# Scans of two head pairs back to back in odd steps, and their decays requested and cleared two at a time

## The reference

```python
xn = layernorm(x)
proj = xn @ in_proj_w.T                        # gate, xBC, dt
xBC = silu(causal_conv4(xBC) + conv_b)         # x (8192 channels), B and C (8 groups of 128)
# scan in chunks of 128 tokens, 128 heads of 64 channels, 16 heads a group
cs = cumsum(dt * A)
scores = einsum('bclhn,bcshn->bchls', C, B) * where(tri, exp(cs_l - cs_s), 0)
y = scores @ (x * dt) + (part from the chunk before) + D * x
yg = y * silu(gate)
out = (yg * rsqrt(mean(yg**2 over a group) + eps)) * norm_w @ out_proj_w.T
return x + out * silu(expert_ffn(xn))
```

## Time and profile before

| | us |
|---|---|
| median of 3 runs (lowest, highest) | 1611.23 (1611.13, 1611.86) |
| profiled execution, its own time | 1611.21 |
| its span | 1609.3 |
| PE busy | 1589.1 |
| DVE busy | 1410.1 |
| ACT busy | 1196.8 |
| POOL busy | 960.9 |

### The profile page before, as it was taken

The page is one execution under the profiler, slowest core; times in us unless marked ns, Lnnn a source line. Parts: engine busy times, 40 slices in busy tenths (PEclk is TensorE's granted clock), DMA queues, the critical chain, the costliest instruction groups (busy, mean ns, idle before and its releaser), DMA issues.

```text
span 1609.3 us, 28461 instructions
## 1 busy us (share of the span) xinstructions
PE 1589.1 (99%) x8478; PEld 1268.0 (79%) x8478; DVE 1410.1 (88%) x1654; ACT 1196.8 (74%) x2305; POOL 960.9 (60%) x596
## 2 busy tenths in 40 slices
PE   9999989999999999999999999999999999999998
PEld 6888768877778777877778777877778777877776
DVE  7726899889898899889898899889998899889987
ACT  4525878777887878777887878777887778778772
POOL 6522456656666656655665656656666656656563
PEclk9999999999999999999999999999999999999999
DMA  5234344434443444434443444334443444434432
GB/s 187 80 130 142 117 142 149 138 113 138 141 152 108 150 133 147 138 114 148 138 144 119 138 134 149 136 115 158 135 139 124 132 134 156 130 120 155 151 132 84
DMA packets 83831, 216.88 MB, mean 135 GB/s; under 512 B 10576, under 2 KB 12880, under 8 KB 83536
## 3 DMA queue, kind: packets, MB, share of 16 engines
q1 hardware_dynamic: 83376, 214.55, 39.7%
q10 hardware_dynamic: 288, 0.30, 0.1%
HBM read 209.83 MB, written 4.98 MB: 133 GB/s over the span
## 4 chain that ended last, share of the span: by engine, by line
PE 86%; DVE 7%; issue 3%; ACT 3%; POOL 1%; DMA 0%; ACTq 0%; DVEq 0%; POOLq 0%; SPq 0%
PE pj L454 15%; PE pj L456 15%; PE pj L455 15%; PE pr L454 9%; PE pr L455 8%; PE pr L456 8%; PE sc L677 7%; PE tb L666 3%; PE sc L681 3%; DVE conv L1335 2%; DVE wo_lo L1399 1%; ACT decay L936 1%; DVE xc L1349 1%; PE tb L690 1%; PE pr L655 1%
## 5 line engine op out<-in xcount | busy, mean ns | idle before, releaser
L1036 POOL TENSOR_TENSOR w_lo<-stg,w_hi 128x512 fp32r<-128x512 f32 x316 | 496.2, 1571 | 322.7 <-ACT w_hi L910 261.4
L454 PE MATMUL pj<-xT_hi,w_hi 128*128 128x512 f32 x1208 | 477.4, 395 | 9.6 <-DVE conv L1335 5.3
L456 PE MATMUL pj<-xT_hi,w_lo 128*128 128x512 f32 x1208 | 471.4, 390 | 0.0
L455 PE MATMUL pj<-xT_lo,w_hi 128*128 128x512 f32 x1208 | 471.0, 390 | 0.0
L1335 DVE SCALAR_TENSOR_TENSOR conv<-pj,par,conv 128x510 f32<-128x510 f32 (+2 forms) x480 | 357.8, 745 | 77.6 <-ACT conv L918 64.4
L936 ACT ACTIVATE decay<-decay,dtg 128x256 f32<-128x256 f32 (+1 forms) x1024 | 379.0, 442 | 0.0
L1073 POOL TENSOR_TENSOR xc<-xc,thg 128x512 f32<-128x512 f32 x128 | 203.1, 1587 | 188.1 <-DVE xc L1386 187.5
L1079 POOL TENSOR_TENSOR sqsum<-sqsum,sq 128x512 f32<-128x512 f32 x112 | 218.1, 1947 | 113.9 <-ACT sq L962 110.5
L454 PEld LDWEIGHTS pj<-xT_hi,w_hi 128*128 128x128 f32 x1208 | 226.9, 188 | 65.5 <-issue 13.5
L456 PEld LDWEIGHTS pj<-xT_hi,w_lo 128*128 128x128 f32 x1208 | 226.9, 188 | 47.9
L455 PEld LDWEIGHTS pj<-xT_lo,w_hi 128*128 128x128 f32 x1208 | 227.1, 188 | 45.1
(11 more groups left out here) (180 smaller groups left out, 1993.2 us busy)
## 6 DMA issues: line engine op xcount, KB each, us to landing
stg<-wstream SPq DMA_DIRECT2D x387, 256.0 KB, 2.7
decay<-cs_scr SPq DMA_DIRECT2D x128, 768.0 KB, 4.3
acc<-hid SPq DMA_DIRECT2D x8, 256.0 KB, 4.6
out<-acc SPq DMA_DIRECT2D x8, 256.0 KB, 2.0
dt_scr<-decay SPq DMA_DIRECT2D x1, 1024.0 KB, 6.5
gate_scr<-part SPq DMA_DIRECT2D x4, 256.0 KB, 2.0
dtg<-dt_scr SPq DMA_DIRECT2D x16, 64.0 KB, 4.5
stg<-hid SPq DMA_DIRECT2D x4, 256.0 KB, 4.5
```

What stands on the lines that cost most here:

```text
L454: nc.tensor.matmul(dst, hi_w, hi_x, start=first, stop=False)
L455: nc.tensor.matmul(dst, hi_w, lo_x, start=False, stop=False)
L456: return nc.tensor.matmul(dst, lo_w, hi_x, start=False, stop=last)
L1036: nc.gpsimd.tensor_tensor(w_dest(n, 1), stg[:, s % RING, :], f32(w_dest(n, 0)), ALU.subtract).then_inc(S["wl"], 1)
```

## The change

PE scans in odd steps only: pair s-1 and pair s back to back. Even pairs still go to the bank `sc`; odd ones go to `tb` (pair 1), `pr[0]` (3) and `pr[3]` (5 and 7), with the waits this needs. In step 1 `x_turn` of pair 2 moves to the end of the step, since `tb` holds pair 1's result. SP requests the decays of pairs s+2 and s+3 in even steps, behind the step's weight tiles. ACT does `drops` of an even pair behind the tap and the second weight split of the even step, and `y_hi` and `square` of two pairs in even steps, the second `square` behind `decays` and ahead of `x_tanh`. POOL and DVE follow: two `add_scan` in odd steps, two `y_lo`, two `add_square` in even ones. `add_output` moves behind the last `x_silu`, and for the fourth tile to the start of step 5.

```diff
+        yb = [sc, tb, sc, pr[0], sc, pr[3], sc, pr[3]]
@@ SP step
-                if has_pair(g, half, s + 3):
-                    load_exponents(*pair(g, half, s + 3))
+                for n in (s + 2, s + 3):
+                    if s % 2 == 0 and has_pair(g, half, n):
+                        load_exponents(*pair(g, half, n))
@@ PE scan
-                pe.wait_ge(S["u"], at(g, half, NJ, j))
+                pe.wait_ge(S["u"], at(g, half, NJ, j - 1))
+                if j == 1:
+                    pe.wait_ge(S["ms"], at(g, half, 1, 0))
+                elif j % 2 == 1:
+                    pe.wait_ge(S["acc"], at(g, half, 4, 1 if j == 3 else 4))
@@ PE step
-                if has_pair(g, half, s + 1):
+                if s != 1 and has_pair(g, half, s + 1):
                     x_turn(*pair(g, half, s + 1))
-                if has_pair(g, half, s):
+                if s % 2 == 1 and has_pair(g, half, s):
+                    scan(g, half, s - 1)
                     scan(g, half, s)
                 if len(mine) > 1:
                     channel_block(g, half, mine[1])
                 if with_out:
                     out_of_step(g, half, s)
+                if s == 1:
+                    x_turn(*pair(g, half, s + 1))
@@ ACT step
-                    if has_pair(g, half, s + 2):
+                    if s % 2 == 1 and has_pair(g, half, s + 2):
                         drops(*pair(g, half, s + 2), 0)
                     gate_tanh(g, half, s)
...
-                if s >= 1 and has_pair(g, half, s - 1):
-                    y_hi(g, half, s - 1)
-                    square(g, half, s - 1)
...
+                if done:
+                    y_hi(*done[0])
+                    square(*done[0])
+                    y_hi(*done[1])
+                if s % 2 == 1 and has_pair(g, half, s + 2):
                     drops(*pair(g, half, s + 2), 1)
                 if mine:
                     tap(g, half, mine[0][1])
                 if i < n:
                     split(g, half, s, i)
                     i += 1
+                if s % 2 == 0 and has_pair(g, half, s + 2):
+                    drops(*pair(g, half, s + 2), 0)
+                    drops(*pair(g, half, s + 2), 1)
                 if has_pair(g, half, s + 2):
                     decays(*pair(g, half, s + 2))
+                if done:
+                    square(*done[1])
                 if mine:
                     x_tanh(*of_half(g, half, mine[0][1]), mine[0][1])
@@ POOL step
                 if with_out and s == 0:
-                    add_square(*before, NJ - 1)
+                    add_square(*before, NJ - 2)
...
                 for i in range(1, n):
                     split_low(g, half, s, i)
-                if has_pair(g, half, s):
+                if with_out and s == 0:
+                    add_square(*before, NJ - 1)
+                if s >= 2 and s % 2 == 0 and has_pair(g, half, s):
+                    add_square(g, half, s - 1)
+                if s % 2 == 1 and has_pair(g, half, s):
+                    gated(g, half, s - 1)
                     gated(g, half, s)
@@ DVE step
-                if has_pair(g, half, s + 1):
+                if s % 2 == 0 and has_pair(g, half, s + 1):
                     x_times_dt(*pair(g, half, s + 1))
-                if has_pair(g, half, s):
+                if s % 2 == 1 and has_pair(g, half, s):
+                    add_scan(g, half, s - 1)
                     add_scan(g, half, s)
+                if s % 2 == 1 and s != 1 and has_pair(g, half, s + 1):
+                    x_times_dt(*pair(g, half, s + 1))
```

More of the change, by code:

```diff
@@ L664, in x_turn @@
                 pe.wait_ge(S["xdt"], at(g, half, NJ, j))
+                if j == 2:
+                    pe.wait_ge(S["u"], at(g, half, NJ, 2))
                 for t in range(4):
@@ L676, in scan @@
                         hd = slice(h * HD, (h + 1) * HD)
-                        nc.tensor.matmul(sc[hd, c0:c0 + 2 * P], xdt[:, j % 2, 2 * b, hd],
+                        nc.tensor.matmul(yb[j][hd, c0:c0 + 2 * P], xdt[:, j % 2, 2 * b, hd],
                                          decay[:, j % NDEC, 2 * h + b, 0:2 * P], start=True, stop=False)
@@ L680, in scan @@
                         hd = slice(h * HD, (h + 1) * HD)
-                        mm = nc.tensor.matmul(sc[hd, c0 + P:c0 + 2 * P], xdt[:, j % 2, 2 * b + 1, hd],
+                        mm = nc.tensor.matmul(yb[j][hd, c0 + P:c0 + 2 * P], xdt[:, j % 2, 2 * b + 1, hd],
                                               decay[:, j % NDEC, 2 * h + b, 2 * P:3 * P], start=False, stop=True)
@@ L705, in out_first @@
                 pe.wait_ge(S["acc"], at(g, half, 4, t + 1))
+                if t in (0, 3):
+                    pe.wait_ge(S["u"], at(g, half, NJ, 4 if t == 0 else NJ))
                 if t == 1 and not is_last(g, half):
@@ L971, in step @@
                         i = 1
-                    if has_pair(g, half, s + 2):
+                    if s % 2 == 1 and has_pair(g, half, s + 2):
                         drops(*pair(g, half, s + 2), 0)
                     gate_tanh(g, half, s)
-                elif has_pair(g, half, s + 2):
+                elif s % 2 == 1 and has_pair(g, half, s + 2):
                     drops(*pair(g, half, s + 2), 0)
-                if s >= 1 and has_pair(g, half, s - 1):
-                    y_hi(g, half, s - 1)
-                    square(g, half, s - 1)
+                before = (g, 0) if half == 1 else (g - 1, 1)
                 if s == 0 and with_out:
[L981 to L984, removed]
+                    done = [(*before, NJ - 2), (*before, NJ - 1)]
+                elif s >= 2 and s % 2 == 0 and has_pair(g, half, s - 1):
+                    done = [(g, half, s - 2), (g, half, s - 1)]
+                else:
+                    done = []
+                if done:
[3 more added lines that the diff above has]
+                if s % 2 == 1 and has_pair(g, half, s + 2):
                     drops(*pair(g, half, s + 2), 1)
@@ L1018, in _ @@
                 step(G - 1, 1, s)
-            y_hi(G - 1, 1, NJ - 1)
-            square(G - 1, 1, NJ - 1)
+            for j in (NJ - 2, NJ - 1):
+                y_hi(G - 1, 1, j)
+                square(G - 1, 1, j)
         @block.gpsimd
@@ L1086, in step @@
                 if with_out and s == 0:
-                    add_square(*before, NJ - 1)
+                    add_square(*before, NJ - 2)
                 if with_out and s == 2:
                     inverse_rms(*before)
-                if s >= 2 and has_pair(g, half, s):
-                    add_square(g, half, s - 1)
+                if s >= 4 and s % 2 == 0 and has_pair(g, half, s):
+                    add_square(g, half, s - 2)
                 for i in range(1, n):
                     split_low(g, half, s, i)
-                if has_pair(g, half, s):
+                if with_out and s == 0:
[4 more added lines that the diff above has]
+                    gated(g, half, s - 1)
                     gated(g, half, s)
@@ L1111, in _ @@
                 step(G - 1, 1, s)
+            add_square(G - 1, 1, NJ - 2)
             add_square(G - 1, 1, NJ - 1)
@@ L1386, in add_scan @@
                 nc.vector.scalar_tensor_tensor(out=xc[:, j, :], in0=xc[:, j, :], scalar=par[:, C_DV + j:C_DV + j + 1],
-                                               in1=sc[:, :], op0=ALU.mult, op1=ALU.add).then_inc(S["u"], 1)
+                                               in1=yb[j][:, :], op0=ALU.mult, op1=ALU.add).then_inc(S["u"], 1)
             def y_lo(g, half, j):
@@ L1424, in step @@
                     mean_square(*before)
+                if with_out and s == 5:
+                    add_output(*before, 3)
                 if has_pair(g, half, s):
@@ L1432, in step @@
                     mask_products(*following(g, half))
-                if has_pair(g, half, s + 1):
+                if s % 2 == 0 and has_pair(g, half, s + 1):
                     x_times_dt(*pair(g, half, s + 1))
-                if has_pair(g, half, s):
+                if s % 2 == 1 and has_pair(g, half, s):
+                    add_scan(g, half, s - 1)
                     add_scan(g, half, s)
+                if s % 2 == 1 and s != 1 and has_pair(g, half, s + 1):
+                    x_times_dt(*pair(g, half, s + 1))
                 for m in mine[1:]:
                     taps(g, half, m)
-                if s >= 1 and has_pair(g, half, s - 1):
-                    y_lo(g, half, s - 1)
+                if s >= 2 and s % 2 == 0 and has_pair(g, half, s - 1):
+                    y_lo(g, half, s - 2)
                 if s == 0 and with_out:
-                    y_lo(*before, NJ - 1)
+                    y_lo(*before, NJ - 2)
                 if mine:
@@ L1448, in step @@
                     split_out_lo(g, half, s)
-                if with_out and 2 <= s <= 5:
-                    add_output(*before, s - 2)
                 for m in mine[1:]:
                     x_silu(*of_half(g, half, m), m)
```

(11 more changed lines are left out.)

## The result

The changed kernel takes 1776.2 us (median of 4, 1770.0 to 1787.8) against 1611.4 before: a ratio of 1.1026, 95% interval 1.1008 to 1.1044. The forecast was 1749 us in 1650 to 1800; 1776 lies at the upper end of that range, just past the 1700 to 1775 that had most of the chances. The profiled execution took 1776.05 us with a span of 1774.1.

A forecast was written before the change was run, and what follows sets the result against it. PE (99% busy) was taken as the bound nearly everywhere, DVE (88%) close behind. New waits less scan savings gave 18.4 us a group, 129 over seven loops, plus 9 outside: 1611.2 + 138 = 1749 us, range 1650 to 1800.

The forecast's parts named there:

- The scans: On PE, two scans back to back pay the switch of weight width once: 0.34 us saved, 64 times, 21.8 us.
- The sum of squares: Step 1: PE waits at `square_sums` for ACT's later square and POOL's add, 2.4 us in half 0, 3.8 in half 1.
- Second taps: Steps 4 and 6 of half 1: the second x block's later tap makes PE wait 1.1 us each, 2.2 together.
- The decays in half 0: Steps 4 and 6: decays requested behind an output tile land late for ACT, delaying step 7's x block, 8.5 us a group.
- W2: Step 4 of half 0: end of `wo_lo` on DVE that frees output tile 2's slot, where the decays' chain starts.
- W4: Step 6 of half 0: the same end of `wo_lo` for output tile 4, forecast at W2 + 31.0 us.
- W2's shift: Half 0: W2 moves back against PE by 1.9 us a group (0 to 2.5), as `x_silu` waits for a later `x_tanh`.
- PE's clock: Rival, 10%: PE runs the block behind two of the waits of about 4 us at half clock, 38 us, total 1787.
- the start: Ahead of the loops: a little, as DVE bounds it already, inside the 9 us added outside the seven loops.
- only the scans count: Rival, 8%: ACT runs ahead so that all late hand-overs hide and the scans' saving remains, 1589 us.
- not late: Rival, 24%: in half 0 SP passes the output tile early enough for the decays; 8.7 us a group, 1676 us.
- only `square_sums` stalls: Rival, 10%: second taps and decays are hidden, leaving the step 1 waits less the scans' saving, 1624 us.

The follow-up runs named there:

- Experiment 1: The changed kernel with decays requested one a step again (pair s+3 in every step), late drops kept: 1715.5 us.
- experiment 7: The kernel before with only the decays' part of the change: requests for two pairs in even steps, late drops of even pairs: 1693.1 us.
- experiments 2 to 4: Changed kernel, second square ahead of the drops (1740.1 us); that with decays requested one a step again (1720.3); the latter, square early in step 0 alone (1704.3).
- experiment 9: Kernel with only the paired scans left (requests and drops as before, second square early), three hand-overs mended (add_output, POOL's add, tail): 1631.0 us.
- experiment 3 to 5: From the changed kernel with decays requested one a step and second square early (1720.3 us) to that with every pair's drops placed as before (1634.9).
- experiment 1 to 6: From the changed kernel with decays requested one a step, second square late (1715.5 us), to that with every pair's drops placed as before (1645.5).
- experiment 10: The mended kernel of paired scans (1631 us), but pairs 4 and 5 scanned in their own steps: 1611.5 us, ratio 0.9990.

## Why the prediction held, and which terms were off

**The scans.** Two in a row cost what was worked out. The transposes of steps 2, 3 and 4 of a half 1, with both scans behind those of step 3:

```profile
904.68 0.60 PE L674 MATMUL tb<-cst,xc 128*128 128x128 f32 x4
913.33 0.60 PE L674 MATMUL tb<-cst,xc 128*128 128x128 f32 x4
...
924.91 0.60 PE L674 MATMUL tb<-cst,xc 128*128 128x128 f32 x4
```

8.65 and 11.58 us, 20.23 for two steps, against two of 10.27 before; that is 0.31 less, forecast 0.34. It does not show as time gained, since PE then waited.

**The sum of squares.** The wait was forecast at 2.4 and 3.8 us a half and is 1.85 and 2.12. Tap to the end of the square was worked out at 6.1 us and takes 6.1:

```profile
976.95 0.78 ACT L936 ACTIVATE conv<-pj,par 128x512 f32<-128x512 f32 x1 [0.65 <-PE pj L461]
...
982.45 0.61 ACT L980 ACTIVATE sq<-xc 128x512 f32<-128x512 f32 x1
...
983.21 1.27 POOL L1107 TENSOR_TENSOR sqsum<-sqsum,sq 128x512 f32<-128x512 f32 x1 [3.29 <-ACT sq L980]
...
984.62 1.05 PE L702 MATMUL tb<-cst,sqsum 128*128 128x1 f32 x8 [1.85 <-POOL sqsum L1107]
```

The add took 1.27 in both halves where I took 1.7. DVE's `x_silu` starts at 983.86, inside the add, and did not lengthen it; the `x_silu` itself took 1.17 us, where one at 1064.45 took 0.68. The Trainium skill's rule (SBUF — State Buffer, "SBUF: two separate sides"), by which the first of the two keeps the ports, gave 1.3 and the trace agrees. The 1.4 us that half 1 was given on top was wrong: `y_hi` of pair 7 was in time, and ACT then waited 0.92 us for PE's x block.

**Second taps.** Forecast 1.1 us in each of steps 4 and 6 of half 1; the waits shown are 1.24 and 1.16. Right.

**The decays in half 0.** W2 was 1020.05 and W4 1049.68, 29.6 apart (forecast 31.0), and the x block started at 1063.28, W2 + 43.2 (forecast 44.6, before 36.1). Requests landed after 4.51 and 4.33 us (forecast 4.3). The loss is 7.1 us and not 8.5. Experiment 1 takes the late request away and ACT no longer waits for a decay; experiment 7 puts late requests and late drops together into the kernel before, and ACT waits for a decay again.

**W2's shift** of 1.9 us did not come: W2 lay 0.60 us ahead of step 4's transposes before, and 0.46 after. DVE's idle time behind the late `x_tanh` is real (2.59 us a wait in step 0), but PE's wait in step 1 had given it back. When that wait was removed, in experiments 2 to 4, PE waited for DVE at step 1's transposes instead; I take that for the same lateness, which no run separates.

**Left out of the sum.** First, `add_output` behind the second `x_silu` holds up the products of B and C, 14.0 us: I gave the move as part of the change and never asked who waits for it. Second, PE's clock. I had it as a rival at 10% and 38 us. In four executions the mean clocks and spans were 0.975 and 1768.1, 0.972 and 1774.1, 0.970 and 1774.3, 0.965 and 1786.1: 18.0 us for 0.010. Carried on to 1.000 that is a span of 1723, so an estimate of some 50 us is the clock's; the slower blocks alone are less, by PE's busy time 37 us. Third, the start: PE waited 7.26 us once at 230.95 for DVE's taps, and 15.4 us were lost there in all where I had put next to nothing.

PE's trace gives the seven groups in three parts, with each gap counted from start to start. Its waits sum to 123.8 us against 3.8 before. The rest of its time is 1280.2 us against 1250.0 in experiment 9, where PE has the same order of work and the clock is 0.996: 30.2 us, nearly all of it the clock. And 1250.0 against 1259.3 before is 9.3 us gained by the scans, where 56 times 0.34 is 19; some 6 of the difference are 42 more restarts of 0.1 us each and one slow stretch in experiment 9, and the rest is not accounted for. Together that is the 140.9.

So the mechanisms were right, but that the total came so near is in part luck, since errors cancel: without the clock my 138 us stands against an estimated 114 to 128 (165 less 50 or 37). The mis-sized terms are `square_sums` (3.97 for 6.2 a group), the decays' chain (7.1 for 8.5) and W2 (0.1 for 1.9); those left out are the clock and `add_output`, and the start was put too low. The rivals "only the scans count", "not late" and "only `square_sums` stalls" are refuted by the waits.

The experiments also correct what I thought was largest. The late drops cost 85 us of the 165 (experiment 3 to 5) or 70 (experiment 1 to 6), more than the request's place (61, measured with the drops late; late requests with early drops were not run). In the sum of the prediction they had no term of their own: they were inside the squares, the second taps and the chain at once. The parts do not add either: removing one lets the next show.

**Still open.** What pairing costs when all else is mended. Experiment 9 is 19 us above before. Undoing two pairs (experiment 10) gave back all 19.5 us, although the wait for the products fell by only some 8 us: the other waits became fewer too. The waits shown are each short by 0.16 us (a matmul's record is 0.39 us, the next starts 0.23 after it). With that added PE's waits over the seven groups are 28.4 us in 51 gaps in experiment 9 and 9.6 us in 22 gaps in experiment 10, which is nearly all of it. By the two profiled executions the three pairings left in experiment 10 pay a little there, 1259.2 us for the seven groups against 1263.1 before, and the last half with the tail is 4.2 us longer. No run tests why.

Nor did any run test the 17.0 us in six places "for nothing that the profile shows". They stand at the first block of the loop body, one at each of the six returns of the loop, 3.7 us at 1030.83. ACT too has 3.0 us of such time there. I take them for PE's own code fetch that its queue no longer covers. That is argued, not shown.

## What to carry to other kernels

When work is moved later on an engine, list every instruction that is now behind it and ask of each, in its own step, who waits for it and since when; the same few microseconds of `drops` made a square, a tanh and a tap late on three different paths. A request that moves behind others in a DMA queue inherits their waits: read from the trace when the piece ahead of it is released, not when the queue is idle. And where PE is at 99%, price each new wait like those here, of 2 to 5 us, twice: once as idle time and once as a slower block that may follow it.

## What was not expected of the hardware

A wait of 3.6 us on PE was followed by a block at half speed (5.29 us for 2.72), and one of 2.12 us in half 1's step 1 by another slow stretch: from `square_sums` to the scan it took 5.40 us at 1088.75 and 3.86 at 984.62, behind a wait of 1.85 us. The length of the wait alone does not decide it: a wait of 2.13 us ahead of the `square_sums` at 1288.34 had no slow stretch behind it.

Executions of the changed kernel also spread over 1%, in step with their mean clocks (0.965 to 0.975), where the four before that were timed beside them agree within 0.05%.
